# Edge products copied to SBUF two batches ahead, gathered rows added by VectorE

## The reference, cut to what matters

```python
edge_input = jnp.concatenate([x[src], edge_attr], axis=-1)
messages = _gelu(edge_input @ mW1 + mb1) @ mW2 + mb2
gates = jax.nn.sigmoid(_gelu(edge_input @ gW1 + gb1) @ gW2 + gb2)
aggregated = jax.ops.segment_sum(messages * gates, dst, num_segments=x.shape[0])
```

## Time and profile before

| | us |
| --- | --- |
| median of 3 runs | 5404.54 |
| lowest, highest | 5398.22, 5406.49 |
| the profiled execution, its own time | 5409.02 |
| its span in the trace | 5407.2 |
| granted TensorE clock, mean over the span | 0.884 |

### The profile page before, as it was taken

How to read it: one execution, slowest core, us unless ns; L and a number is a source line. 1 busy time by engine, 2 the same in 40 slices (tenths; PEclk the granted TensorE clock), 3 DMA queues, 4 the chain that set the end, 5 groups by cost and what they waited for, 6 DMA issues and landing times.

```text
span 5407.2 us, 94817 instructions
## 1 busy us (share of the span) xinstructions
PE 4217.6 (78%) x35340; PEld 2569.2 (48%) x35340; DVE 3456.3 (64%) x5455; ACT 2200.9 (41%) x4155; POOL 3239.7 (60%) x2920
## 2 busy tenths in 40 slices
PE   4899899999965566656666565656479999999999
PEld 3888899999943333323333332323333333333333
DVE  6999533544344444444444444444379999999999
ACT  4999200101011111111111111111168888888887
POOL 3699100000046666666666666666358888888888
PEclk9999999999977777787777777777689999999999
DMA  3344899698833334343344344343111221122121
GB/s 71 162 195 195 323 363 370 252 397 336 327 97 113 116 117 120 120 120 113 119 121 120 111 123 119 118 121 111 36 42 57 58 63 57 57 66 57 57 64 38
DMA packets 296568, 760.27 MB, mean 141 GB/s; under 512 B 81160, under 2 KB 183752, under 8 KB 289992
## 3 DMA queue, kind: packets, MB, share of 16 engines
q1 hardware_dynamic: 217496, 595.47, 30.3%
q0 software_dynamic: 78768, 160.85, 11.1%
HBM read 589.77 MB, written 166.38 MB: 140 GB/s over the span
## 4 chain that ended last, share of the span: by engine, by line
PE 55%; another core or an unknown queue 16%; issue 14%; DVE 7%; ACT 4%; POOL 2%; DMA 1%; DVEq 1%; SPq 0%; ACTq 0%; POOLq 0%
PE p_e L1167 15%; PE p_tr L1325 10%; PE p_e L1310 9%; PE p_e L1199 4%; PE p_e L1209 4%; PE p_mm L1287 3%; PE p_tr L1209 2%; ACT GA L1601 2%; PE p_tr L1199 2%; POOL VA L788 1%; PE p_mm L1098 1%; DVE VA L2417 1%; PE p_tr L1026 1%; PE p_mm L1209 1%
## 5 line engine op out<-in xcount | busy, mean ns | idle before, releaser
L788 POOL DMA_INDIRECT GA<-table_mg,VA x1568 | 1493.2, 952 | 1720.0 <-DMA table_mg<-VA 957.8
L2417 DVE TENSOR_TENSOR VA<-VA,p_mm 128x1024 f32<-128x1024 f32 (+1 forms) x1204 | 1362.2, 1208 | 6.1 <-POOL VA L902 5.0
L902 POOL TENSOR_SCALAR VA<-VA 128x1024 f32<-128x1024 f32 (+1 forms) x1204 | 1235.9, 1045 | 168.7 <-ACT VA L1655 155.8
L1199 PE MATMUL p_e<-BD,EA 128*128 128x384 f32 x896 | 467.5, 610 | 492.2 <-ACT GA L1601 266.9
L1655 ACT ACTIVATE VA<-p_e 128x1024 f32<-128x1024 f32 x602 | 616.0, 1023 | 178.1 <-PE p_e L1310 174.5
L1325 PE MATMUL p_tr<-VA,GA 128*32 128x512 f32 (+1 forms) x5096 | 641.3, 580 | 2.7 <-ACT GA L1675 2.1
L1601 ACT ACTIVATE GA<-p_e 128x384 f32<-128x384 f32 x448 | 214.8, 490 | 985.9 <-remote 601.1
L2264 DVE SCALAR_TENSOR_TENSOR R<-R,keep,M 128x97 f32<-128x97 f32 x1568 | 512.6, 327 | 126.1 <-issue 11.7
L2246 DVE TENSOR_TENSOR M<-GA,p_mm 128x1344 f32<-128x1344 f32 x112 | 174.1, 1554 | 653.1 <-issue 348.2
L1199 PEld LDWEIGHTS p_e<-BD,EA 128*128 128x128 f32 x896 | 193.6, 232 | 712.4 <-issue 383.4
L1310 PE MATMUL p_e<-T,GA 32*128 32x512 f16 x4632 | 443.4, 379 | 1.8 <-DVE GA L2386 1.1
(11 more groups left out here) (265 smaller groups left out, 6552.3 us busy)
## 6 DMA issues: line engine op xcount, KB each, us to landing
GA<-adj SPq DMA_DIRECT2D x98, 800.0 KB, 6.1
VA<-adj SPq DMA_DIRECT2D x98, 800.0 KB, 6.2
run_m<-R SPq DMA_DIRECT2D x112, 700.0 KB
GA<-adj SPq DMA_DIRECT2D x98, 768.0 KB, 6.1
VA<-adj SPq DMA_DIRECT2D x98, 768.0 KB, 6.1
H<-adj SPq DMA_DIRECT2D x56, 896.0 KB, 5.1
adj<-GA SPq DMA_DIRECT2D x25, 1568.0 KB, 5.3
adj<-VA SPq DMA_DIRECT2D x24, 1568.0 KB, 5.3
```

The costliest lines, as they stand in the source:

```text
L788: pool.indirect_dma_start(out=to, out_offset=None, in_=of, in_offset=bass.IndirectOffsetOnAxis(ap=at, axis=0)).then_inc(s, 16)
L902: pool.tensor_scalar(e, e, HIGH, LOW, ALU.min, ALU.max).then_inc(clipped, 1)
L1199: mm = pe.matmul(p_h[k][0:CH, 0:4 * D], EA[:, n % 2, k // 2, :], BD[:, 2 * (k % 2):2 * (k % 2) + 2, :, :].rearrange("p a b f -> p (a b f)" ...
L2417: dve.tensor_tensor(e, e, p_mm[n % 2][:, 0:cols_of(n)].unsqueeze(1).to_broadcast([P, 2, cols_of(n)]), ALU.mult).then_inc(weighed, 1)
```

## The change

TensorE makes the edge products alone and posts `edge_product` after each, using 8 PSUM banks. ScalarE copies each bank to SBUF (`keep_edges`, L1580, 7 for a batch) into one of four slots `hid` (three in GA, one in VA), two batches ahead of the rows. VectorE adds the gathered rows to the slot in two halves of 128x1344 (`add_rows`, L2235) and posts `rows_added`; ScalarE applies Gelu to each half in place (L1591). VectorE now runs the sums of batch n-1 between the addition for batch n and its messages. `gate_row` and `gates` move from PSUM to SBUF. POOL waits once for a batch, for the additions of batch n-2, and all 14 gathers of a batch post to one semaphore.

```diff
@@ POOL, sum_pass
                 for k in range(2 * ITER):
+                    wait(pool, rows_added, 2 * (k - 1))
                     for j in range(U):
-                        if j % 2 == 0:
-                            wait(pool, hidden_ready, BANKS * (k - 2) + j // 2 + 1)
-                        gather(G[0:CH, k % 2, j, 0:2 * D], table_mg, sources[:, U * k + j:U * k + j + 1],
-                               rows_landed[k % 2][j // 2])
+                        gather(rows[:, k % 2, j, :], table_mg, sources[:, U * k + j:U * k + j + 1], rows_landed[k % 2])
@@ TensorE, sum_pass
-                for m in range(LEAD):
-                    edges(m)
-                for m in range(BANKS * BATCHES):
-                    rows(m)
-                    if m + LEAD < BANKS * BATCHES:
-                        edges(m + LEAD)
-                pe.wait_ge(gelu_done, BANKS * BATCHES)
+                for m in range(BANKS * BATCHES):
...
+                    wait(pe, edges_kept, m - len(p_h) + 1)
+                    pe.matmul(p_h[m % len(p_h)][0:CH, 0:4 * D], EA[:, n % 2, k // 2, :],
+                              BD[:, 2 * (k % 2):2 * (k % 2) + 2, :, :].rearrange("p a b f -> p (a b f)"),
+                              start=True, stop=True).then_inc(edge_product, 1)
+                pe.wait_ge(edges_kept, BANKS * BATCHES)
@@ ScalarE, sum_pass
+                def keep_edges(n):
+                    wait(act, sums_ready[n % 2], (n - SLOTS_E) // 2 + 1)
+                    for k in range(BANKS):
+                        m = BANKS * n + k
+                        act.wait_ge(edge_product, m + 1)
+                        act.activation(hid[n % SLOTS_E][:, 2 * k:2 * k + 2, :],
+                                       p_h[m % len(p_h)][0:CH, 0:4 * D].rearrange("p (a f) -> p a f", a=2), ACT.Copy
+                                       ).then_inc(edges_kept, 1)
+                for n in range(AHEAD_E):
+                    keep_edges(n)
+                for n in range(BATCHES):
+                    for c in (0, 1):
+                        half = hid[n % SLOTS_E][:, BANKS * c:BANKS * (c + 1), :]
+                        act.wait_ge(rows_added, 2 * n + c + 1)
+                        act.activation(half, half, ACT.Gelu).then_inc(gelu_done, 1)
                     act.wait_ge(logit_ready, n + 1)
                     act.activation(gates, small[:, 0, 0:U], ACT.Tanh, bias=half_bias, scale=0.5).then_inc(gate_ready, 1)
+                    if n + AHEAD_E < BATCHES:
+                        keep_edges(n + AHEAD_E)
@@ VectorE, sum_pass
+                def add_rows(n):
+                    dve.wait_ge(edges_kept, BANKS * (n + 1))
+                    dve.wait_ge(rows_landed[n % 2], 16 * U * (n // 2 + 1))
+                    for c in (0, 1):
+                        half = hid[n % SLOTS_E][:, BANKS * c:BANKS * (c + 1), :]
+                        dve.tensor_tensor(half, half, rows[:, n % 2, BANKS * c:BANKS * (c + 1), :], ALU.add
+                                          ).then_inc(rows_added, 1)
+                def messages(n):
+                    both = hid[n % SLOTS_E]
...
+                    dve.wait_ge(gelu_done, 2 * (n + 1))
+                    dve.tensor_tensor(M[:, :, 0:D], both[:, :, D:2 * D], gate_row.unsqueeze(1).to_broadcast([CH, U, D]),
...
+                                             in1=both[:, :, 0:D], op0=ALU.add, op1=ALU.mult)
+                for n in range(BATCHES):
+                    add_rows(n)
+                    if n:
+                        run_sums(n - 1)
+                    messages(n)
+                run_sums(BATCHES - 1)
@@ PSUM and SBUF
-        gate_row = p_mm[1][0:CH, 0:D]
-        gates = p_mm[1][0:CH, D:D + U]
+        gate_row = gw2[0:CH, :]
+        gates = small[:, 1, 0:U]
@@ SyncE, load_batch
                     if k >= 2:
-                        sp.wait_ge(edge_product, k - 1)
+                        sp.wait_ge(edge_product, BANKS * (k - 1))
```

More of the change, by code:

```diff
@@ L44 @@
 ROOM = 16
-LEAD = 4
-GATE_AT = 1
-assert LEAD < BANKS
+AHEAD_E = 2
+SLOTS_E = 4
 MW = D + 1
@@ L343, in build @@
         p_e = [p_four[:, k, :] for k in range(4)]
-        p_h = [*p_e, *p_tr, p_mm[0]]
+        p_h = [*p_e, *p_tr, *p_mm]
         p_pair = p_four[:, 0:2, :]
@@ L347, in build @@
         p_sums = p_tr[0]
-        gate_row = p_mm[1][0:CH, 0:D]
-        gates = p_mm[1][0:CH, D:D + U]
+        gate_row = gw2[0:CH, :]
+        gates = small[:, 1, 0:U]
+        rows = GA[0:CH, 0:2 * U * 2 * D].rearrange("p (h u f) -> p h u f", h=2, u=U)
+        hid_at = [*[GA[0:CH, (2 + k) * U * 2 * D:(3 + k) * U * 2 * D] for k in range(SLOTS_E - 1)], VA[0:CH, 0:U * 2 * D]]
+        hid = [a.rearrange("p (u f) -> p u f", u=U) for a in hid_at]
+        assert (SLOTS_E + 1) * U * 2 * D <= GA.shape[1] and U * 2 * D <= TILES * D
         half_bias = small[:, 2, 0:1]
@@ L405, in build @@
         sources_landed = sem("sources_landed")
-        hidden_ready = sem("hidden_ready")
+        rows_landed = [sem(f"rows_landed{h}") for h in (0, 1)]
+        edges_kept = sem("edges_kept")
+        rows_added = sem("rows_added")
         sums_ready = [sem(f"sums_ready{h}") for h in (0, 1)]
@@ L436, in build @@
         rows_cleared, spares_stored, open_added = combined, comb_ready, edge_added
[L437 to L440, removed]
+        scattered = [[sem(f"scattered{n}_{a}") for a in range(ACCS)] for n in range(ATTEND + 1)]
         acc_landed = [sem(f"acc_landed{k}") for k in range(PIECES)]
@@ L1590, in sum_pass @@
             def sum_pass():
-                def gate_of(n):
+                def keep_edges(n):
[6 more added lines that the diff above has]
+                                       ).then_inc(edges_kept, 1)
+                act.wait_ge(table_stored, 16 * GROUPS * 2)
+                for n in range(AHEAD_E):
[5 more added lines that the diff above has]
+                        act.activation(half, half, ACT.Gelu).then_inc(gelu_done, 1)
                     act.wait_ge(logit_ready, n + 1)
                     act.activation(gates, small[:, 0, 0:U], ACT.Tanh, bias=half_bias, scale=0.5).then_inc(gate_ready, 1)
[L1596 to L1602, removed]
-                                       ).then_inc(gelu_done, 1)
-                        if n and k == GATE_AT:
-                            gate_of(n - 1)
-                gate_of(BATCHES - 1)
+                    if n + AHEAD_E < BATCHES:
+                        keep_edges(n + AHEAD_E)
             def scatter_pass(n):
@@ L2235, in sum_pass @@
             def sum_pass():
-                dve.tensor_copy(gate_row, gw2[0:CH, :])
                 dve.tensor_scalar(half_bias, sc[0:CH, 1:2], 0.5, None, ALU.mult)
                 dve.drain()
-                for n in range(BATCHES):
-                    h = n % 2
+                def add_rows(n):
[7 more added lines that the diff above has]
+                    both = hid[n % SLOTS_E]
                     dve.drain()
-                    dve.wait_ge(gelu_done, BANKS * (n + 1))
-                    hid = A[0:CH, h, :, :]
-                    dve.tensor_tensor(M[:, :, 0:D], hid[:, :, D:2 * D], gate_row.unsqueeze(1).to_broadcast([CH, U, D]),
+                    dve.wait_ge(gelu_done, 2 * (n + 1))
+                    dve.tensor_tensor(M[:, :, 0:D], both[:, :, D:2 * D], gate_row.unsqueeze(1).to_broadcast([CH, U, D]),
                                       ALU.mult)
@@ L2251, in sum_pass, with run_sums @@
                     dve.scalar_tensor_tensor(out=M[:, :, 0:D], in0=gates.unsqueeze(2).to_broadcast([CH, U, D]), scalar=1.0,
-                                             in1=hid[:, :, 0:D], op0=ALU.add, op1=ALU.mult)
+                                             in1=both[:, :, 0:D], op0=ALU.add, op1=ALU.mult)
                     dve.tensor_scalar(M[:, :, D:MW], gates.unsqueeze(2), 1.0, None, ALU.add)
+                def run_sums(n):
+                    h = n % 2
                     for j in range(U):
```

1 line of the change is left out of this document (removed).

## The result

The changed kernel took 5465.93 us (median of 3, 5463.88 to 5479.24) against 5404.54 before: 61 us more, ratio 1.0129 with the interval 1.0107 to 1.0152. The forecast was 5695. The profiled execution spans 5464.0 us, 56.8 more than before.

- The first gather starts 4.5 us earlier.
- The gathers run from 1519.8 to 3843.35 us, 2323.6 us against 2255.4, +68.1.
- From the last gather's start to L831 it is 22.7 us against 32.8, -10.1.
- All behind L831 is 3.3 us longer.

A forecast was written before the change was run, and what follows sets the result against it. POOL's gather stream, stopped by late TensorE posts, was taken as the bound: 17.56 + 4.4 (stops) + 0.8 (lengthened gathers) = 22.8 us a batch against 20.14, +290 us with head and tail, giving 5695 us; range 5290 to 5900.

The forecast's parts named there:

- What bounds the kernel now: Edge stage: POOL's gathers pace it at 17.56 us a batch, plus 2.58 us of stops from late TensorE posts.
- Streaming lets through 17.56 / 10, under 2: TensorE's posts: each batch needs 7, but under 2 get through while POOL streams, so ScalarE's copies fall behind.
- What a stop costs: POOL restarts only after a whole addition: 9.5 to 15.5 us every 3 to 3.5 batches, taken as 4.4 a batch.
- VectorE's wide operations beside gathers: Edge stage: additions and messages with two SBUF inputs lengthen gathers by 0 to 2.8 us a batch, taken as 0.8.
- VectorE and ScalarE no bound: Edge stage: VectorE needs 13 to 14 us a batch and ScalarE 6.1, both under POOL's 17.56.
- Tail: Behind the last gather: one and a half batches of Gelus and messages remain instead of some 2.5, -10 us.
- Head: Start of the edge stage: the third batch's gathers wait for copies, table load and two additions, +3 us.
- The second one: Edge stage: no lag but the full lock, 20.36 us a batch, 5422 us, or 5265 with half the lock; chance 0.13.
- The first rival: Edge stage: the lag goes with the row matmuls or POOL's waits on TensorE, 17.56 us a batch, 5109 us; chance 0.13.

The follow-up runs named there:

- Groups 2 and 4: Two groups of follow-up runs, each on one chip with the kernel before, whose traces show no "remote" waits; the kernel before took 5074 and 5068 us.
- e5: Kernel before with a tiny memset (128x8) on POOL ahead of every fifth gather; 5085 us, ratio 1.0012.
- e4: Kernel before with TensorE posting `hidden_ready` once a batch, after the last row product, and doing 7 edge, then 7 row products; 5395 us, ratio 0.9989.
- e1: Changed kernel with `gate_row` and gates put back into PSUM, leaving 7 banks for products; 5479 us, ratio 1.0141 to the kernel before.
- e18: Kernel before with three memsets of 128x512 (0.54 us) a batch on POOL between gathers; 5412 us, ratio 1.0008.

## Why the prediction was wrong

*What bounds the kernel now* was right: POOL's stream of 17.56 us a batch plus stops, and the stops are TensorE's late posts. Groups 2 and 4 show it best: there the kernel before takes 5074 and 5068 us, 330 and 336 less than 5404.54. It was not traced there, but e5 was, whose pauses cost nothing. It has no remote wait, 277 us less in the edge stage's gathers, 16 less from the last gather to L831, and 30 less behind that, where posts are late as well. The reading was incomplete, since I took the lateness for a property of the kernel that the change would inherit.

*"Streaming lets through 17.56 / 10, under 2", and with it "What a stop costs": this step failed.* As many posts as before must come, seven a batch, but they no longer come late. I took 4.4 us a batch for stops; in the whole stage POOL made one, of 29.8 us, 0.27 a batch. I had read the earlier trace rows as a rate at which posts are served, and e4 shows that it is none. What kept the posts prompt in the changed kernel is its own hold-ups, as far as the runs show. L2243 and L2248 break POOL's stream for 1 us each, 3.5 us apart. SyncE's load of the attributes, which TensorE waits for, goes out at about the same time, once the sums are stored (2498.91 in the same timeline, beside L2243 at 2498.60). So every run of products in the timeline after 1600 us begins at most 6.5 us after the end of a hold-up of that size, though up to 17 us pass from one such pair to the next with only the additions' 0.6 us between. Beside the gathers of the first two batches, where none of these operations stand yet, posts are late in the changed kernel too:

```profile
1549.46 0.56 DVE L2136 TENSOR_TENSOR T<-p_mm,B 128x384 f32<-128x384 f32 x1 [14.93 <-remote]
...
1557.14 0.59 ACT L1512 ACTIVATE hT<-p_tr 96x512 f32<-96x512 f32 x1 [19.07 <-remote]
```

e1 shows it from the other side: with the hold-ups of these two taken away the late posts are back. That it was their timing, and not their sum with the additions (3.0 us a batch), is my reading; see behind e18.

*"VectorE's wide operations beside gathers"*: right in kind, taken too small. The bounds were 0 and 2.8 us; 0.8 was taken, and 2.74 came in longer gathers and 0.26 in held-up starts, 3.0 together. This term, and not the stops, made the kernel slower. That the time came out above the old one, as forecast, and inside 5290 to 5900, is luck: with stops of 0.27 us a batch, as they were, my 0.8 would have given a faster kernel. The reason for the choice ("the stops swallow part") fell with the stops, and the nearness to the running sums was no reason. Worked out from the gathers of the earlier trace rows, the upper end was the right one. The page "SBUF — State Buffer" of the Trainium skill, section "SBUF: two separate sides", says that a VectorE operation with two SBUF inputs and a GpSimd operation that reads SBUF lock each other out, each for its whole instruction. The trace agrees for wide operations, gathers of 1.90 and 2.00 us beside 1.56 us each, and shows nothing of it beside the 0.32 us running sums or beside the reduction L2246, which has one input.

*VectorE and ScalarE no bound*: right; 150 and 77 of 250 us busy. *Tail* -10: -10.1. *Head* +3: the third batch started 64.7 us after the first gather against 54.9, +9.7, because POOL waited for both additions, and VectorE began them only behind its L2166 of the stage before, which ended at 1580.79 us; ScalarE's copies were there by then.

*The rivals.* The second one, no lag but every wide operation holding gathers up, is what happened in this stage: it gave 5422. It had 20.36 us a batch in all, where 20.53 came. It also set this beside 20.14, which has POOL's first stop of 20.10 us in it, and left out the changed kernel's own of 29.8 us. With both, worked out afterwards, the stage comes to 112 x 20.53 + 29.8 = 2329, less some 6 for the first two batches, whose gathers meet nothing: 2323, as measured, and the time to 5404.5 + 68 - 10 = 5462. It had 0.13 of the chance. What it lacked was a reason for the lag to go; the earlier trace rows show posts freed once POOL stood still, and a hold-up of POOL by VectorE is a short stand too. The first rival (5109) gave the time of a kernel with neither, near what the kernel before itself takes in the prompt groups; its condition, that the lag goes with the row matmuls, is answered by e1.

## What to carry to other kernels

Two stalls of one stage can be tied: what lengthens one may be the cure of the other, so removing one and pricing the other at its old size counts neither rightly; look for the event that ends a stall before multiplying it. Beside a stream of indirect DMAs, count the wide VectorE operations with two inputs in SBUF: about 1 us here for each message operation, and 0.6 to 3.1 us for the two additions. Taking one operand back to PSUM shortened the gathers (e1) but not the time in a late group, where stops took the place of the hold-ups; what it would give in a prompt one was not measured. And time the kernel before more than once, in separate groups: here it had two levels 6% apart, and a comparison across groups would have shown a gain or a loss that no edit made.

## What the runs showed of the hardware that was not expected

With gathers in an unbroken stream (one each 1.254 us), posts of TensorE reached ScalarE, VectorE and POOL late (14 to 19 us in half the batches of e4) in three of five groups of runs, and in the other two never, with one chip in both kinds. The same kernel in the same order of work took 5397 to 5420 us and 5068 to 5074, so nothing in the code decides it; what does stays open. Gathers landed within 2.6 us of their issue in the late groups and up to 8.4 us behind it in the prompt ones. Breaks of 0.97 us ahead of every fifth gather ended the lateness, of 0.54 and 0.12 us did not, and whether the length of a break or the sum in a batch counts is not shown. A memset of 128x8 between two gathers took no time from the stream, one of 128x1024 took 0.84 us, and a drain on POOL between gathers 2.0 to 4.6 us.

No version beat the kernel before in either kind of group. The nearest was e4 in a late one, 0.9989 (0.9976 to 1.0002), which is no clear gain.
